# Low one-hots on ScalarE from the read result, and the histogram transfers on SyncE

## The reference

```python
ub = concat(table_i1[his[:, :, 0]], table_i2[his[:, :, 1]], table_i3[his[:, :, 2]])   # [B, 200, 96]
mask = his[:, :, 0] == 0
h = concat(q, ub, q - ub, q * ub) @ w_att1.T + b_att1
score = where(mask, 0, h @ w_att2.T + b_att2)
browse = einsum('bl,ble->be', score, ub)
x = dice(concat(item_emb, browse, user_emb) @ w1.T + b1)
x = dice(x @ w2.T + b2)            # dice takes mean and variance over all 2048 users
return sigmoid(x @ w3.T + b3)
```

## Time and profile before

| | us |
|---|---|
| median of three runs | 1507.39 |
| lowest and highest | 1504.2, 1511.55 |
| span of the profiled execution | 1506.3 |
| busy: DVE, PE, POOL, ACT | 1405.9, 1299.2, 1188.4, 758.1 |
| picks (all 512), first to last start | 48.8 to 1444.6 |

### The profile page before, as it was taken

How to read it: one execution, slowest core, us unless ns; L and a number is a source line. 1 busy time by engine, 2 the same in 40 slices (tenths; PEclk the granted TensorE clock), 3 DMA queues, 4 the chain that set the end, 5 groups by cost and what they waited for, 6 DMA issues and landing times.

```text
span 1506.3 us, 66273 instructions
## 1 busy us (share of the span) xinstructions
PE 1299.2 (86%) x27007; PEld 1186.0 (79%) x27007; DVE 1405.9 (93%) x1397; ACT 758.1 (50%) x1729; POOL 1188.4 (79%) x1671
## 2 busy tenths in 40 slices
PE   5688989889898988889898998989899898988864
PEld 4577878888887988788788888878888887888761
DVE  6699999999999999899999999999999999999945
ACT  5554455555445555454555554454555545452217
POOL 3588788888888888788888888888888888888830
PEclk8899999999999999999999999999999999999966
DMA  3566676666667666666766666666676666565820
GB/s 51 111 137 127 127 143 133 141 144 141 124 137 143 130 146 140 127 133 133 143 131 142 146 141 134 130 137 132 143 143 140 141 132 138 131 149 133 153 54 1
DMA packets 517508, 194.38 MB, mean 129 GB/s; under 512 B 485445, under 2 KB 493237, under 8 KB 517245
## 3 DMA queue, kind: packets, MB, share of 16 engines
q1 hardware_dynamic: 499654, 162.61, 53.5%
q10 hardware_dynamic: 15448, 26.51, 6.7%
q0 software_dynamic: 2144, 1.36, 0.8%
HBM read 8.45 MB, written 1.44 MB: 7 GB/s over the span
## 4 chain that ended last, share of the span: by engine, by line
POOL 72%; issue 15%; PE 3%; DVE 3%; POOLq 3%; ACT 2%; DMA 1%; ACTq 1%; SPq 0%; DVEq 0%
POOL score L439 24%; POOL score_r L448 14%; POOL score L444 11%; POOL parts L449 9%; POOL parts L452 6%; POOL item_rows L417 4%; POOL parts L445 3%; POOL user_rows L425 2%; DVE score_j L1026 1%; DVE onehot_lo L1012 1%; ACT scores_b L775 1%; PE sel L727 1%; DMA hiT<-onehot_hi 1%; POOLq L437 1%; POOLq L443 1%
## 5 line engine op out<-in xcount | busy, mean ns | idle before, releaser
L560 PE MATMUL wsum_ps<-scaled_lo,onehot_hi 100*128 100x75 bf16 x12288 | 535.0, 201 | 81.5 <-DVE scaled_lo L1038 80.2
L543 PEld LDWEIGHTS sel<-scoretab,hiT 128*128 128x128 bf16 x12288 | 495.8, 99 | 121.6 <-DMA hiT<-onehot_hi 59.2
L543 PE MATMUL sel<-scoretab,hiT 128*128 128x75 bf16 x12288 | 534.5, 201 | 63.1 <-DMA hiT<-onehot_hi 43.9
L1038 DVE TENSOR_TENSOR scaled_lo<-onehot_lo,parts 100x3744 bf16<-100x3744 bf16 x256 | 539.0, 2105 | 34.4 <-POOL parts L452 26.4
L560 PEld LDWEIGHTS wsum_ps<-scaled_lo,onehot_hi 100*128 100x128 bf16 x12288 | 486.1, 99 | 106.3 <-DVE scaled_lo L1038 101.7
L439 POOL TENSOR_TENSOR score<-score_j 100x16 f32<-100x16 f32 x256 | 386.6, 1510 | 156.6 <-DVE score_j L1026 155.7
L768 ACT ACTIVATE wsum_ring<-wsum_ps 128x300 f32<-128x300 f32 x512 | 215.5, 421 | 525.7 <-PE wsum_ps L560 497.2
L1026 DVE TENSOR_REDUCE score_j<-sel 100x24 f32<-100x600 f32 x512 | 395.5, 772 | 21.0 <-PE sel L543 21.0
L994 DVE TENSOR_TENSOR onehot_hi<-digits,iota_hi 100x1920 bf16<-100x1920 bf16 x256 | 296.1, 1157 | 3.4 <-PE wsum_ps L560 3.3
L775 ACT ACTIVATE scores_b<-acc 128x512 bf16<-128x512 f32 (+1 forms) x318 | 255.4, 803 | 50.0 <-issue 22.7
L448 POOL TENSOR_TENSOR score_r<-score,parts 100x16 f32<-100x16 f32 x256 | 207.3, 810 | 20.0
(11 more groups left out here) (168 smaller groups left out, 724.0 us busy)
## 6 DMA issues: line engine op xcount, KB each, us to landing
scoretab<-scores_b SPq DMA_DIRECT2D x384, 93.8 KB
weightsum<-wsum_ring ACTq DMA_DIRECT2D x128, 125.0 KB
weightsum<-wsum_ring ACTq DMA_DIRECT2D x64, 150.0 KB
raw<-in_r_rec_his_dram SPq DMA_DIRECT2D x32, 150.0 KB
hiT<-onehot_hi SPq DMA_TRANSPOSE x256, 3.8
x_rows<-x_tile SPq DMA_DIRECT2D x14, 100.0 KB
scores_b<-x_rows SPq DMA_DIRECT2D x1, 1400.0 KB
item_rows<-in_L_rec_table_i_dram,ids_now POOLq DMA_INDIRECT x51
```

Source lines behind the costliest of these rows:

```text
L543: mm = pe.matmul(sel[:, 2 * (s % 2) + q, (c % 4) * W:(c % 4 + 1) * W] .rearrange("p (j v) -> p j v", j=NF), hiT[0:HJ, s // 2 % 4, g * POSP ...
L560: mm = pe.matmul(wsum_ps[:, s % 2, b * W:(b + 1) * W].rearrange("p (j v) -> p j v", j=NF), hi_columns(ring_slot(n), g), scaled_lo[:, n % 2 ...
L1038: ins = dve.tensor_tensor(scaled_lo[:, n % 2, :, :, :].rearrange("p q i (u d) -> p (q i) u d", d=2), onehot_lo[:, n % 2, :, :, :].rearrang ...
```

## The change

ScalarE makes the low one-hots. As the read result is the score at v = lo and at or below -FAR elsewhere, Relu(x / FAR + 1) is 1 there and 0 elsewhere. The operation reads the same two PSUM banks as pick, half a step at a time, and pick now waits for it and no longer for PE. onehot_low leaves DVE. `onehot_lo` has four buffers in place of two and rows of 76 (75 and one zero column) in place of 3 x 26; `scaled_lo` has 76 columns too. The low digits themselves are no longer kept; the task that took them out of PSUM writes lo - 12 and its square at once (`rims`, two operations for one), and lo_rows becomes one copy. collect_sums moves from ACT's order into SP's: the quarters of a tile are issued in steps 8, 11 and 15 and in step 3 of the next tile, after that step's transpose and place_scores.

```diff
 # ScalarE
+            def onehot_low(t, s):
+                k = t * SLOTS + s
+                n, g0 = s // 2, (s % 2) * 8
+                if s % 2 == 0 and not (isinstance(k, int) and k < 2 * LOWS):
+                    act.wait_ge(scaled_ready, t * STEPS + n - LOWS + 1)
+                act.wait_ge(sel_full, k + 1)
+                act.activation(onehot_lo[:, n % LOWS, g0:g0 + 8, 0:W].rearrange("p (q c) u -> p q c u", q=2),
+                               sel[0:POS, 2 * (s % 2):2 * (s % 2) + 2, 0:4 * W].rearrange("p q (c u) -> p q c u", u=W),
+                               ACT.Relu, bias=one[:, :], scale=1.0 / FAR).then_inc(lo_ready, 1)
             def slot(t, s, odd, last=False):
                 here = tasks_of(t)
+                onehot_low(t, s)
...
-                if s in (4, 5, 6) and not (isinstance(t, int) and t == 0):
-                    collect_sums(t - 1, 3, s - 4)
-                for w, first in enumerate((16, 20, 28)):
-                    if first <= s < first + NF:
-                        collect_sums(t, w, s - first)
...
-                act.activation(rows[:, :, :, 0], low, ACT.Identity, bias=centre[:, :])
-                act.activation(rows[:, :, :, 1], low, ACT.Square, bias=centre[:, :]).then_inc(lo_rows_ready, 1)
+                act.activation(onehot_hi[0:POS, ring_slot(n), :, 1:1 + 2 * NF],
+                               rims[:, hb, g0:g0 + PER, :, :].rearrange("p g j i -> p g (j i)"), ACT.Copy
+                               ).then_inc(lo_rows_ready, 1)
...
+                        act.activation(rims_j[:, :, :, 0], src, ACT.Identity, bias=centre[:, :])
+                        ins = act.activation(rims_j[:, :, :, 1], src, ACT.Square, bias=centre[:, :])
 # SyncE
+            def collect_sums(t, w):
+                k = 4 * t + w
+                await_ge(wsum_copied, 8 * k + 8)
+                if not (isinstance(k, int) and k < 1):
+                    await_ge(weightsum_in, NF * 16 * k)
+                if w == 0 and not (isinstance(t, int) and t == 0):
+                    await_ge(task_full, task_before(t, FIN_SLOT + PARTS - 1) + 1)
+                for j in range(NF):
+                    r = slice(hi_first(j) if j else 0, hi_first(j) + HI)
+                    sp.dma_start(weightsum[r, w, :, :]..., wsum_ring[r, w % 2, ...]...).then_inc(weightsum_in, 16)
 # tile, after turn_hi and place_scores of step n
+                    if n == 3 and not (isinstance(t, int) and t == 0):
+                        collect_sums(t - 1, 3)
+                    if n in (8, 11, 15):
+                        collect_sums(t, (8, 11, 15).index(n))
 # TensorE, read_scores
                 if not (isinstance(k, int) and k < 2):
+                    pe.wait_ge(lo_ready, k - 1)
                     pe.wait_ge(score_ready, k - 1)
 # VectorE
-            def onehot_low(t, n):
...
             def pick(t, s):
-                dve.wait_ge(sel_full, k + 1)
+                dve.wait_ge(lo_ready, k + 1)
             def scale(t, n):
-                dve.wait_ge(lo_ready, k + 1)
+                dve.wait_ge(lo_ready, 2 * k + 2)
             def step(t, n, last=False):
...
-                onehot_low(t, n)
```

More of the change, by code:

```diff
@@ L35, in build @@
     HB = 8
-    LP = LO + 1
-    HJ, U, W = HB + NF * HI, NF * LP, NF * LO
+    HJ, W = HB + NF * HI, NF * LO
+    U = W + 1
     TILE, HALF = 128, 64
@@ L46, in build @@
     HELD = 4
+    LOWS = 4
     MH = H1 // 2
@@ L77, in build @@
         parts = sb("parts", [POS, 2, PER, 3, 2], BF16)
-        digits = sb("digits", [POS, 2, 2, 2 * HALF, NF, 2], BF16)
+        digits = sb("digits", [POS, 2, 2 * HALF, NF, 2], BF16)
+        rims = sb("rims", [POS, 2, 2 * HALF, NF, 2], BF16)
         far_rows = sb("far_rows", [1, 3, LO], BF16)
@@ L94, in build @@
         iota_hi = sb("iota_hi", [POS, HI], BF16)
-        iota_lo = sb("iota_lo", [POS, LP], BF16)
+        iota_lo = sb("iota_lo", [POS, LO], BF16)
+        one = sb("one", [POS, 1])
         identf = sb("identf", [128, 128])
@@ L355, in keep_x1 @@
                 sp.dma_start(x1_rows[:, :, bass.ds(t * TILE, TILE)], x1_tile[:, :, :]).then_inc(x1_out, 16)
+            def collect_sums(t, w):
[7 more added lines that the diff above has]
+                    r = slice(hi_first(j) if j else 0, hi_first(j) + HI)
+                    sp.dma_start(weightsum[r, w, :, :].rearrange("p l b -> p (l b)"),
+                                 wsum_ring[r, w % 2, j * LO:(j + 1) * LO, :].rearrange("p l b -> p (l b)")
+                                 ).then_inc(weightsum_in, 16)
             def tile(t, odd, last=False):
@@ L478, in _ @@
             chain(pool.tensor_copy(iota_hi[:, :], iota_i[:, :]))
-            chain(pool.iota(iota_i[:, 0:LP], pattern=[[1, LP]], base=-LO, channel_multiplier=0))
-            chain(pool.tensor_copy(iota_lo[:, :], iota_i[:, 0:LP]))
+            chain(pool.iota(iota_i[:, 0:LO], pattern=[[1, LO]], base=-LO, channel_multiplier=0))
+            chain(pool.tensor_copy(iota_lo[:, :], iota_i[:, 0:LO]))
             column = far_column[:, :]
@@ L803, in task @@
                         else:
[L804 to L808, removed]
+                            act.wait_ge(lo_rows_ready, (t - 1) * STEPS + 8 * hb + 8)
+                    src = (misc_b if kind == 1 else misc)[0:POS, 0:2 * NF * HALF].rearrange("p (j g) -> p j g", j=NF)
+                    if kind == 1:
+                        ins = act.activation(digits[:, hb, :, :, :].rearrange("p g j d -> p j g d"),
+                                             src.unsqueeze(3).to_broadcast([POS, NF, 2 * HALF, 2]), ACT.Copy)
+                    else:
+                        rims_j = rims[:, hb, :, :, :].rearrange("p g j i -> p j g i")
+                        act.activation(rims_j[:, :, :, 0], src, ACT.Identity, bias=centre[:, :])
+                        ins = act.activation(rims_j[:, :, :, 1], src, ACT.Square, bias=centre[:, :])
                 elif name == "item":
@@ L832, in task @@
                 ins.then_inc(task_copied, 1)
[L834 to L847, removed]
             def scale_raw(h, taken):
@@ L946, in _ @@
                 copy_sums(TILES - 1, s)
-            for j in range(NF):
-                collect_sums(TILES - 1, 3, j)
             for i, what in enumerate(FIN):
@@ L994, in onehot_high @@
                 dve.tensor_tensor(onehot_hi[0:POS, ring_slot(n), :, HB:].rearrange("p g (j v d) -> p g j v d", j=NF, d=2),
-                                  digits[:, hb, 1, g0:g0 + PER, :, :].unsqueeze(3)
+                                  digits[:, hb, g0:g0 + PER, :, :].unsqueeze(3)
                                   .to_broadcast([POS, PER, NF, HI // 2, 2]),
@@ L1076, in _ @@
             dve.memset(offset[:, :], -float(MID) / LO).then_inc(bias_ready, 1)
+            dve.memset(one[:, :], 1.0).then_inc(bias_ready, 1)
+            dve.memset(onehot_lo[:, :, :, W:U], 0.0).then_inc(bias_ready, 1)
             dve.memset(w2col[:, :], 0.0).then_inc(dve_tail_pre, 1)
```

11 lines of the change are left out of this document (5 added, 6 removed).

## The result

The changed kernel takes 1560.12 us (median of 4 runs, 1554.37 to 1572.69) against 1506.53 for the kernel before beside it: a ratio of 1.0367, 95% interval 1.0332 to 1.0401. It is slower by 54 us; 1380 was forecast. The profiled execution has a span of 1552.5 us. The kernel before was run again beside each experiment and had 1505.2 to 1506.5 us each time. One kernel, e1_collect_act, has a slower state in three of its ten executions (1506.11 is the median of all ten, the 1506 of the later expectations); its time is given as the median of the seven others, 1502.05.

The account below looks back on a forecast made before the run. DVE bounds the kernel at 87.4 us a tile and the bound passes to PE: 75.5 + finish 2.0 + ACT 1.5 + POOL 0.5 + light steps 0.5 make 80.0 us, so 1380 us, range 1325 to 1445.

Parts of the forecast that it names:

- DVE's light step: One step on VectorE without onehot_low: from 5.23 us to 4.43, a tile of 71.7 us.
- The low one-hot: On ScalarE, 100x600 f32 out of PSUM, 32 a tile: 0.70 us each, 0.94 at the upper price.
- PE's own work: TensorE's matmuls in a tile, summed from single groups: 74.7 us, plus 1 for the clock, 75.5 as stated.
- finish waits for the transfers: Slot 9 on PE: the last quarter, issued in step 3, lands late; 2.0 us a tile, bounds 0 and 4.
- transposes late: SyncE's transpose after step 8's burst starts 1 us late, with 2 of cover; nothing in the sum, bounds 0 and 1.
- waits for ScalarE's copies: 0.5 us a tile for low one-hots late after scale_raw, 1.0 for PE's waits on split copies no longer hidden.
- light steps and POOL: 0.5 us a tile for steps 13 to 15 and 0 at DVE's pace, 0.5 for POOL's gathers.
- Point 5 of the change: Twelve collecting transfers a tile move to SyncE, about 43 to 51 us of a tile; finish waits 2.0 us.
- a sign of being wrong: PE waiting on hiT transposes for more than the 43.9 us of the kernel before.
- three of the four bursts: On SyncE, three bursts fit between two transposes; step 8's doesn't, needing 5.9 us against a step of 5.
- rival C: Slower, 1520 to 1570 us: SyncE's bursts delay transposes, each adding 2.1 us issue and up to 2.1 landing; chance 0.07.
- Point 2: ScalarE's tile: low one-hots add 22.4 us, two rims for one copy 0.4, row operations save 3.5; 65 us.

Follow-up runs that it names:

- e1_collect_act: Changed kernel with the twelve collecting transfers of a tile back in ScalarE's order: 1502.05 us, ratio 0.9973 to the kernel before.
- e3_both: Changed kernel with collecting on ScalarE's queue and plain low digits, leaving only the move of the low one-hots: 1448.84 us, ratio 0.9639.
- e6: Changed kernel with the last quarter collected in SyncE's step 2, ahead of the table pieces, and plain low digits: 1500.72 us, ratio 0.9971.
- e2: Changed kernel with low digits taken by one plain copy and lo_rows made of two small operations, collecting still on SyncE: 1533.08 us, ratio 1.0189.
- e5: Changed kernel with the last quarter collected in SyncE's step 2, ahead of the table pieces, not at the end of step 3: 1525.75 us.
- e11: The kernel of e6 with SyncE's first load of raw ids in step 1 in place of step 2: 1483.22 us, ratio 0.9823.
- e8: The kernel of e1_collect_act with the two rim operations walking position by position and feature by feature: 1451.61 us, ratio 0.965.
- e9: The kernel of e8 with SyncE's first load of raw ids in step 1 in place of step 2: 1440.84 us, ratio 0.9583.
- e10: The kernel of e9 with ScalarE's raw operations in slots 11 and 28 in place of 8 and 23: 1447.21 us, ratio 0.9618.
- e12: The kernel of e10 with the split pieces of rounds 3 to 6 starting three slots earlier: 1446.56 us, ratio 0.9614.

## Why the prediction was wrong

**Right.** DVE bounds the kernel before and POOL only follows it. Taking onehot_low away brings DVE's light step to 4.42 us. The low one-hot costs 0.76 us, and with the link through ScalarE alone the kernel is faster (e3_both). The bound passes to PE. Finish waits for the last quarter, 14 times. All of that came, and the sign was wrong, because the terms that were to be small were not. The sum by its own terms, us a tile over the 14 tiles, and the same for e3_both, where the two mistakes below are undone and the forecast would be 78.0:

| term | forecast | measured | off | e3_both |
|---|---|---|---|---|
| PE's own work | 75.5 | 78.6 | 3.1 | 77.2 |
| finish waits for the transfers | 2.0 | 4.0 | 2.0 | 0 |
| transposes late | 0 | 3.8 | 3.8 | 2.9 |
| waits for ScalarE's copies | 1.5 | 3.1 | 1.6 | 2.4 |
| light steps and POOL | 1.0 | 1.5 | 0.5 | 1.7 |
| tile | 80.0 | 91.0 | 11.0 | 84.2 |

(The tile is (1403.03 - 129.67) / 14, from the picks that open tile 1 and tile 15; PE's own work is that less 173.2 / 14. For e3_both it is (1305.97 - 127.25) / 14 and 97.6 us of waits.)

**Point 5 of the change failed**, the transfers. It named the wait of finish and gave it 2.0 us with 4 as the bound. I started SyncE's step 3 from the end of onehot_high, as if SyncE were free then. It was still at the table pieces and raw ids of step 2 until 971.8, the transpose took 2.29 in place of 1.5, and the landing came 3.0 after the third issue in place of 2.7; the third transfer left 8 us after the step's first pick and not 5.

The same point put the late transposes at nothing, although has 43.9 us of such waits before the change (2.4 us a tile of them over the 14 tiles), and gave them 2 us of cover, more than there was. They are 71.2 us in the changed kernel, a sign of being wrong that the prediction named. It said that three of the four bursts fit between two transposes. In the trace of the kernel before, the issue of a transpose ends 1.8 to 2.2 us after its onehot_high in every step (means of 14 tiles). In the changed kernel it ends 3.4 us after it behind the burst of step 15, 3.1 behind that of step 3, 3.5 behind that of step 8 and 2.4 behind that of step 11; with the transfers back on ScalarE (e1_collect_act) it is 1.8 to 2.0 for the same four. PE waits for the last two: 1.1 us a tile in slot 22 and 0.5 in slot 28. It is the issue that is late. From issue to landing, where the trace tells it, a transpose takes 3.7 us in the median and 7.2 at most, where the earlier trace rows has 3.8 and 6.7; the landing of up to 2.1 us that rival C added to each burst did not show.

The runs put the price of the whole move at 58 to 84 us. With plain digits, the 84 are 32 for the quarter of step 3 (e6 against e2; 34 by e5 against the changed kernel), 17 for raw ids behind transfers (e11 against e6; they came up only when the quarter moved) and 34 for what is left, transposes above all (e11 against e3). This is rival C's place and engine, which I gave 0.07, and the 1560 lie between its 1520 and 1570. Its mechanism was right in one half, the transpose issued late behind three collects; the other half of the price is the wait that I had in my sum at half its size.

**Point 2 failed on a minor operation.** I gave the two rims 0.4 us extra a tile and looked only at element counts; they cost 4.9 us of ScalarE in slots 3 and 21, and 27 to 53 us of the run (e8, which changes their order alone, gives 50). The line for the 100x768 copy, 0.85 us, is a price for its own pattern, in which each value is written twice, side by side.

**PE's own work** was counted at the full granted clock with 1 us added. Over these tiles it is 78.6, and by the same subtraction 87.65 - 123.4/14 = 78.8 before. The busy time of 78.9, which I set aside as too high, was right within 0.1, and the sum from single groups 3 us too low; which groups it priced too low was not found out. The wait in slot 9 cost more than its own length: after 4.83 us of it 3.3 us of work ran at a granted clock of 0.50, and the sum at 981.10 took 1.73 us for 1.01. The 69 us more at the lower level cost up to 34 us by my estimate, if PE worked all through them and work there takes twice its time.

**The remaining distance.** Without the two mistakes the gain is 56 us (e3_both), 65 with the cheap repair of the raw ids (e9), not 127. The last column of the table has the rest: 6.2 us a tile over the 78.0, where the changed kernel is 11.0 over its 80.0. Of the 6.2, 2.9 are the transposes put at nothing, 1.7 PE's own work, 0.9 copies and 0.7 scales. PE's waits there are not one cause: e10 and e12 removed two more of them and the time stayed. How far below 1441 the order could be brought was not found out.

## What to carry to other kernels

When the engine that bounds a kernel is relieved and the next one is 10% behind it, sum the next one's own time from a window less its waits, and expect that a queue that was late but hidden becomes a wait: PE waited 34.2 us for hiT over 14 tiles before the change and 52.9 after it. Move transfers between queues only after writing down what the new queue is doing at that moment, not what it does on average: SyncE had 35 free us a tile by the prediction's count and still sent the third transfer 3 us late. Price an operation by a row that reads and writes in the same pattern (the same rims took 1.56 and 1.72 us in one order and 0.69 in the other), and measure a change with three parts as three kernels: here one part gained 56 us and two lost 111.

## What the runs showed that was not expected

- ScalarE writing 384 bf16 values a partition one halfword at a time, 12 bytes apart, reading PSUM in order: 1.56 us (Identity) and 1.72 (Square). In the other loop order, written 4 bytes apart and read 512 bytes apart, 0.69 for both.
- In the changed kernel, after a wait of 4.83 us, PE's granted clock was 0.50 for the next 3.3 us, and 24 matmuls took 1.73 us where they take 1.01.
- Two costs on different engines overlapped by 26 us: the slow rims cost 53 us alone (e1_collect_act against e3_both) and 27 beside the late transfers (the changed kernel against e2_digits_plain).
